# Last stage of a fused transformer layer: the router's products laid between another product's blocks, and the order of VectorE's work behind them

## What is computed

```python
x = x + ao
xf = _rms(x, n2_w).reshape(-1, C)
logits = jnp.nan_to_num(xf @ gate_w.T)
probs = jax.nn.softmax(logits, axis=-1)
topv, topi = jax.lax.top_k(probs, K)                 # K = 2 of E = 4
topv = topv / (topv.sum(-1, keepdims=True) + 1e-08)
wts = jnp.zeros((N, E), x.dtype).at[jnp.arange(N)[:, None], topi].add(topv)
o0 = _gelu(xf @ e0_up.T) @ e0_down.T
o1 = _silu(xf @ e1_w1.T) * (xf @ e1_w2.T) @ e1_down.T
o2 = _gelu(_gelu(_gelu(xf @ e2_l1.T) @ e2_l2.T) @ e2_l3.T) @ e2_l4.T
o3 = _gelu(_gelu(xf @ e3_down.T) @ e3_up.T) @ e3_out.T
moe = wts[:, 0:1] * o0 + wts[:, 1:2] * o1 + wts[:, 2:3] * o2 + wts[:, 3:4] * o3
```

## Time and profile before

| what | value |
|---|---|
| time, median of 3 runs | 5092.77 us (5092.59 to 5112.78) |
| span of the profiled execution | 5116.3 us |
| mean granted TensorE clock | 0.934 of full speed |
| busy share of the span: TensorE, VectorE, ScalarE, GpSimd | 93%, 78%, 56%, 5% |
| the last stage | about 4380 to 5116 us |

### The profile page before, as it was taken

The page is one execution under the profiler, slowest core; times in us unless marked ns, Lnnn a source line. Parts: engine busy times, 40 slices in busy tenths (PEclk is TensorE's granted clock), DMA queues, the critical chain, the costliest instruction groups (busy, mean ns, idle before and its releaser), DMA issues.

```text
span 5116.3 us, 82733 instructions
## 1 busy us (share of the span) xinstructions
PE 4781.3 (93%) x31872; PEld 2539.4 (50%) x31872; DVE 4006.1 (78%) x9075; ACT 2867.2 (56%) x3349; POOL 241.8 (5%) x259
## 2 busy tenths in 40 slices
PE   6699997868999999999999999999999999899999
PEld 5455555754434344433334433334443333688888
DVE  8677775767898988888888989988899875555555
ACT  4356554433566766666666667666567677332232
POOL 5200001110000000000000000000000000300000
PEclk9799898877899999999999999999899999899999
DMA  6622223765000201200300300300300000210010
GB/s 192 175 77 69 65 51 105 230 221 97 16 11 14 48 16 32 43 9 5 50 13 21 58 9 5 50 13 20 54 11 8 9 7 7 71 42 21 21 42 9
DMA packets 259185, 258.36 MB, mean 50 GB/s; under 512 B 78288, under 2 KB 198096, under 8 KB 257440
## 3 DMA queue, kind: packets, MB, share of 16 engines
q1 hardware_dynamic: 250784, 212.86, 14.8%
q0 software_dynamic: 6240, 38.80, 4.7%
q10 hardware_dynamic: 1768, 1.42, 0.2%
HBM read 145.44 MB, written 105.97 MB: 49 GB/s over the span
## 4 chain that ended last, share of the span: by engine, by line
PE 73%; DVE 19%; issue 5%; ACT 2%; SPq 1%; DMA 1%; DVEq 0%; ACTq 0%
PE psum L885 24%; PE psum L813 20%; PE psum L76 14%; DVE maxes_dense L951 11%; PE psum L845 4%; PE psum L777 3%; PE psum L802 2%; PE psum L823 1%; PE psum L854 1%; PE psum L1656 1%; DVE masked_scores_dense L944 1%; PE psum L809 1%; PE psum L1636 0%; PE psum L864 0%; ACT probs_dense L908 0%
## 5 line engine op out<-in xcount | busy, mean ns | idle before, releaser
L908 ACT ACTIVATE probs_dense<-psum 128x1024 f32<-128x1024 f32 (+3 forms) x2304 | 2068.1, 950 | 1042.2 <-PE psum L845 755.1
L951 DVE TENSOR_REDUCE maxes_dense<-psum 128x1 f32<-128x512 f32 x3584 | 2227.5, 684 | 232.1 <-PE psum L813 231.3
L813 PE MATMUL psum<-keys,queries_dense 48*128 48x512 f32 (+3 forms) x4608 | 1553.0, 477 | 114.6 <-DVE maxes_dense L951 22.1
L813 PEld LDWEIGHTS psum<-keys,queries_dense 48*128 48x128 f32 x4608 | 668.2, 191 | 1471.4 <-DVE maxes_dense L951 1143.6
L885 PE MATMUL psum<-probs_dense,values 128*32 128x512 f32 (+3 forms) x9216 | 1181.2, 591 | 0.0
L845 PE MATMUL psum<-queries_dense,keys 50*128 50x512 f32 (+3 forms) x4608 | 809.7, 407 | 11.5 <-ACT probs_dense L908 11.2
L944 DVE CUSTOM_DVE_ANT_0 masked_scores_dense<-psum,causal_add 128x128 f32<-128x128 f32 (+3 forms) x1024 | 452.4, 488 | 151.5 <-PE psum L813 132.2
L845 PEld LDWEIGHTS psum<-queries_dense,keys 50*128 50x128 f32 x4608 | 449.6, 193 | 106.4 <-ACT probs_dense L908 60.0
L944 DVE CUSTOM_DVE_ANT_0 masked_scores_sparse<-psum,after_add 128x512 f32<-128x512 f32 x512 | 326.2, 687 | 99.9 <-PE psum L802 99.0
L1763 ACT ACTIVATE activated<-psum 128x512 f32<-128x512 f32 x208 | 124.4, 598 | 417.5 <-PE psum L76 405.8
L885 PEld LDWEIGHTS psum<-probs_dense,values 128*32 128x32 f32 x9216 | 189.9, 109 | 273.1 <-issue 203.0
(11 more groups left out here) (296 smaller groups left out, 5252.6 us busy)
## 6 DMA issues: line engine op xcount, KB each, us to landing
v_scratch<-ve_s SPq DMA_DIRECT2D x96, 256.0 KB, 3.5
queries_dense<-parts_scratch SPq DMA_DIRECT2D x384, 64.0 KB
keys<-parts_scratch POOLq DMA_DIRECT2D x42, 512.0 KB, 18.0
parts_scratch<-part_high SPq DMA_DIRECT2D x16, 1024.0 KB, 4.3
parts_scratch<-part_low SPq DMA_DIRECT2D x16, 1024.0 KB, 7.1
values<-v_scratch POOLq DMA_DIRECT2D x8, 2048.0 KB, 35.3
queries_sparse<-parts_scratch SPq DMA_DIRECT2D x192, 64.0 KB
own_keys<-parts_scratch SPq DMA_DIRECT2D x192, 64.0 KB
```

The lines of the kernel that those rows point to most:

```text
L813: m = pe.matmul(bank[:, 0:width], q[rows(h, TROWS), h // 2, b * P:(b + 1) * P], k[rows(h, TROWS), h // 2, kc * STRIP:kc * STRIP + width], ...
L908: act.activation(probs[i % 6][:, :, first_col:STRIP], psum[:, at2:at2 + 2, first_col:STRIP], ACT.Exp, scale=SCALE, **extra).then_inc(exp_d ...
L951: m = dve.tensor_reduce(mx[:, h * BLOCKS + b, kc:kc + 1], bank, AX.X, ALU.max)
```

## The change

- TensorE: `router` becomes `router(s, b)`, one block of 6 matmuls. `expert_out(s, 2)` calls it for the next strip behind each of its four blocks. Block 0 waits for `xft_split`.
- PSUM: the router's results go to `router_bank`, which is bank 0, the first half of `turn_bank`. The router has no entry in `o_order` any more, so its wait for an output bank is gone and the experts' blocks follow one another in the two output banks.
- Semaphores: the router's last block counts `end_turned` up, which so gets 4 counts for each strip where it had 3; the waits on it are counted anew. `combine` on TensorE waits for `logit_ready` of the strip before where it waited for `xft_split`.
- VectorE: `router` is cut in two. `router_logits` (three instructions, up to `logit_ready`) stays ahead of `expert_out` 3; `router_weights` (the rest) comes behind it. The instructions are the same. For strip 0 the order is as it was.

```diff
-        turn_bank = psum[:, 0:2, :]
+        turn_bank, router_bank = psum[:, 0:2, :], psum[:, 0, :]
...
-            o_order += [(2, s, b) for b in range(BLOCKS)]
-            if s + 1 < STRIPS:
-                o_order.append(("router", s + 1, 0))
-            o_order += [(3, s, b) for b in range(BLOCKS)]
+            o_order += [(e, s, b) for e in (2, 3) for b in range(BLOCKS)]
...
                 if s >= 1:
-                    pe.wait_ge(xft_split, s)
+                    pe.wait_ge(logit_ready, s)
                 turn(ao2)
...
-            def router(s):
-                k = o_at["router", s, 0]
-                pe.wait_ge(xft_split, s + 1)
-                pe.wait_ge(o_freed, k - 1)
-                for b in range(BLOCKS):
-                    m = products(pe, o_bank(k)[:, b * EXPERTS:(b + 1) * EXPERTS], lambda l, c: xft[l][:, c, b * P:(b + 1) * P],
-                                 lambda r, c: w["gate_w"][r][:, c, :], DC)
-                m.then_inc(o_filled, 1)
+            def router(s, b):
+                if b == 0:
+                    pe.wait_ge(xft_split, s + 1)
+                m = products(pe, router_bank[:, b * EXPERTS:(b + 1) * EXPERTS], lambda l, c: xft[l][:, c, b * P:(b + 1) * P],
+                             lambda r, c: w["gate_w"][r][:, c, :], DC)
+                if b == BLOCKS - 1:
+                    m.then_inc(end_turned, 1)
...
                              lambda r, c: w[name][r][:, c, :], HC).then_inc(o_filled, 1)
+                    if e == 2 and s + 1 < STRIPS:
+                        router(s + 1, b)
...
-            router(0)
+            for b in range(BLOCKS):
+                router(0, b)
...
                 expert_out(s, 2)
-                if s + 1 < STRIPS:
-                    router(s + 1)
                 expert_out(s, 3)
...
-            def router(s):
-                k, weights = o_at["router", s, 0], wts[s % 2]
+            def router_logits(s):
                 big = 3.4028234663852886e38
+                dve.wait_ge(end_turned, 4 * s + 4)
+                chain.then(dve.tensor_scalar(logit[:].rearrange("p b e -> p (b e)"), router_bank[:, 0:BLOCKS * EXPERTS],
+                                             big, -big, ALU.min, ALU.max))
+                chain.settle()
+                chain.then(dve.tensor_reduce(red[:, :, 0], logit[:], AX.X, ALU.max))
+                chain.settle()
+                dve.tensor_tensor(logit[:], logit[:], bcast(red[:, :, 0], EXPERTS), ALU.subtract).then_inc(logit_ready, 1)
+
+            def router_weights(s):
+                weights = wts[s % 2]
                 flat = "p b e f -> p (b e f)"
-                dve.wait_ge(o_filled, k + 1)
-                dve.tensor_scalar(logit[:].rearrange("p b e -> p (b e)"), o_bank(k)[:, 0:BLOCKS * EXPERTS],
-                                  big, -big, ALU.min, ALU.max).then_inc(o_freed, 1)
-                dve.wait_ge(o_freed, k + 1)
-                chain.then(dve.tensor_reduce(red[:, :, 0], logit[:], AX.X, ALU.max))
-                chain.settle()
-                dve.tensor_tensor(logit[:], logit[:], bcast(red[:, :, 0], EXPERTS), ALU.subtract).then_inc(logit_ready, 1)
                 dve.wait_ge(prob_ready, s + 1)
...
                 expert_out(s, 2)
                 if s + 1 < STRIPS:
-                    router(s + 1)
+                    router_logits(s + 1)
                 expert_out(s, 3)
+                if s + 1 < STRIPS:
+                    router_weights(s + 1)
```

More of the change, by code:

```diff
@@ L1584, in _build @@
         hid_at = lambda s, layer: hids[(len(layers) * s + layer) % 3]
-        o_order = [("kept", 0, 0), ("kept", 0, 1), ("proj", 0, 0), ("proj", 0, 1), ("router", 0, 0)]
+        o_order = [("kept", 0, 0), ("kept", 0, 1), ("proj", 0, 0), ("proj", 0, 1)]
         for s in range(STRIPS):
@@ L1606, in load_end @@
                 if s >= 1:
-                    sp.wait_ge(end_turned, 3 * (s - 1) + 1)
+                    sp.wait_ge(end_turned, 4 * (s - 1) + 1)
                 sp.dma_start(ao2[:], rows_of(ao_d[2], s)).then_inc(ao2_in, 16)
@@ L1612, in load_end @@
                 if s >= 1:
-                    sp.wait_ge(end_turned, 3 * (s - 1) + 2)
+                    sp.wait_ge(end_turned, 4 * (s - 1) + 2)
                 sp.dma_start(ao1[:], rows_of(ao_d[1], s)).then_inc(ao1_in, 16)
@@ L1732, in combine @@
             def combine(s):
-                act.wait_ge(end_turned, 3 * s + 1)
+                act.wait_ge(end_turned, 4 * s + 1)
                 if s >= 1:
@@ L1736, in combine @@
                 act.activation(a2t[:], turn_bank, ACT.Copy).then_inc(features_set, 1)
-                act.wait_ge(end_turned, 3 * s + 2)
+                act.wait_ge(end_turned, 4 * s + 2)
                 if s >= 1:
@@ L1744, in high_norm @@
             def high_norm(s):
-                act.wait_ge(end_turned, 3 * s + 3)
+                act.wait_ge(end_turned, 4 * s + 3)
                 if s >= 1:
                     act.wait_ge(h_done, per_h * (s - 1) + first_h[5])
-                    act.wait_ge(o_filled, o_at["router", s - 1, 0] + 1)
+                    act.wait_ge(end_turned, 4 * s)
                 act.activation(xft[0][:], turn_bank, ACT.Copy).then_inc(features_set, 1)
@@ L1804, in combine @@
                 if s >= 1:
-                    dve.wait_ge(end_turned, 3 * s)
+                    dve.wait_ge(end_turned, 4 * s - 1)
                 for b in range(BLOCKS):
@@ L1825, in low_norm @@
                 dve.tensor_tensor(xft[1][:], turn_bank, xft[0][:].bitcast(F32), ALU.subtract).then_inc(xft_split, 1)
-            def router(s):
-                k, weights = o_at["router", s, 0], wts[s % 2]
+            def router_logits(s):
                 big = 3.4028234663852886e38
-                flat = "p b e f -> p (b e f)"
-                dve.wait_ge(o_filled, k + 1)
-                dve.tensor_scalar(logit[:].rearrange("p b e -> p (b e)"), o_bank(k)[:, 0:BLOCKS * EXPERTS],
-                                  big, -big, ALU.min, ALU.max).then_inc(o_freed, 1)
-                dve.wait_ge(o_freed, k + 1)
+                dve.wait_ge(end_turned, 4 * s + 4)
+                chain.then(dve.tensor_scalar(logit[:].rearrange("p b e -> p (b e)"), router_bank[:, 0:BLOCKS * EXPERTS],
+                                             big, -big, ALU.min, ALU.max))
+                chain.settle()
                 chain.then(dve.tensor_reduce(red[:, :, 0], logit[:], AX.X, ALU.max))
@@ L1837, in router @@
                 dve.tensor_tensor(logit[:], logit[:], bcast(red[:, :, 0], EXPERTS), ALU.subtract).then_inc(logit_ready, 1)
+            def router_weights(s):
+                weights = wts[s % 2]
+                flat = "p b e f -> p (b e f)"
                 dve.wait_ge(prob_ready, s + 1)
@@ L1917, in experts_dve @@
             low_norm(0)
-            router(0)
+            router_logits(0)
+            router_weights(0)
             for s in range(STRIPS):
```

## The result

The changed kernel takes 5119.43 us (median of 20 runs, 5099.65 to 5139.6) against 5095.66 us for the kernel before (20 runs, 5071.83 to 5122.38). The ratio is 1.0034, with a 95% interval of 1.0020 to 1.0048: slower by 10 to 24 us, 17 by the ratio (the medians alone lie 23.8 apart), and within the 0.5% that the prediction calls no change. 5119.43 lies in the prediction's whole range (5074 to 5121), but above the forecast's own (5090 to 5112), at the lower end of what rival B was to give (5119 to 5127).

A forecast was written before the change was run, and what follows sets the result against it. TensorE's timeline, its idle time and clock, was taken to bound the stage. Boundaries save 17.8 us with the clock up, falls add 7.4 each at 3 or 4: +8 on 5092.77 gives 5101, own range 5090 to 5112, whole 5074 to 5121.

The forecast's parts named there:

- rival B: Clock down at nearly every boundary, six or seven of seven: +26.6 to +34 us, 5119 to 5127; chance 0.16.
- Step 1: Expert 3's wait at a boundary goes with the banks read in turn: four blocks take 5.36 not 7.69, 2.33 us saved.
- Step 2: Expert 2's third block no longer waits for VectorE's reading of the first: 0.28 us saved a boundary.
- Step 3: New TensorE wait for xft_low before the first router block, behind expert 2's first block: 1.30 us lost a boundary.
- Step 4: The router's 24 instructions keep their 2.68 us on TensorE: cost 0, bounds -0.1 and +0.2 a switch.
- Step 5: VectorE's 3.47 us weights chain, now behind expert 3, delays no TensorE product: cost 0, 2.3 us of cover.
- Step 7: TensorE's clock falls behind the new wait and thinned expert 2 blocks at 3 or 4 boundaries, 7.4 us each.
- k: Number of the seven boundaries where the clock falls; taken as half, 3 or 4, giving +4.4 or +11.8 us.
- price of 0.48 for a slow microsecond: Each microsecond of slow TensorE clock lengthens a boundary by 0.48 us, from the fourth and sixth boundaries before.
- Rival A: No or one clock fall, only idle time counting: -17.8 to -10.4 us, 5075 to 5082; chance 0.22.
- C: The weights chain reaches TensorE: 7 times up to 3.47, +24 us on top of Rival A, 5099 to 5107; chance 0.07.
- D: Expert 3's wait stays because something other than the router chain held it: +7 us, 5100; chance 0.05.

The follow-up runs named there:

- e7: e3_later with VectorE's eight rank comparisons made four times over, lengthening the weights chain; 5073.89 us in a single run.
- e8: e3_later with VectorE's eight rank comparisons made seven times over, lengthening the weights chain further; 5111.95 us in a single run.
- e4_together: The changed kernel with all four router blocks together behind expert 2's last block, VectorE's new order and the other bank kept; 0.9966 of the kernel before.
- e5_pair: The changed kernel with router blocks one expert block later, the last two side by side behind expert 2's fourth block; 5109.31 us in a single run.
- e2_wide: The changed kernel with every router matmul multiplying 192 columns of expert weights in place of 4, the wait kept; 5108.80 us in a single run.
- e3_later: The changed kernel with each router block placed one expert block later, the last behind expert 3's first block; 0.9933 of the kernel before.
- e1_fill: The changed kernel with expert 2's first block computed twice at each boundary, filling the wait for xft_low; 0.9965 of the kernel before.

## Why the prediction was right, step by step

The mechanism and each wait were right. The size was low: +8, against 14.5 in the trace and 10 to 24 in the times. The median 5119.43 is 18.4 above the 5101 forecast: 2.9 because the kernel before now takes 5095.66 where its first three runs gave 5092.77, 6.5 because the boundaries lost 14.5 and not 8, and 9.0 that one profile doesn't explain.

- Step 1, expert 3's wait gone: right. From expert 3's first load to layer 0's is 4758.78 - 4753.42 = 5.36 us at a boundary with the clock up, the forecast to the digit.
- Step 2, expert 2's wait gone: right; no weight load there waits but for `xft_low`.
- Step 3, the new wait of 1.30: right (4746.72 - 4745.31 - 0.11 = 1.30).
- Step 4, the router at its old pace: right, since the pieces add up to 20.2 as forecast (20.15 to 20.21).
- Step 5, the weights chain hidden with 2.3 us of cover: right; the chain ended 4762.84 - 4743.97 - 0.11 = 18.76 us after the first block began, for 18.75 forecast, and e7 and e8 measured the cover.
- Step 7, the clock: the kind was right, and both of its terms were too small. Four of seven fell, the upper of the "3 or 4"; the falls began 3.5 to 3.7 us into the boundary, where the prediction had 3 to 6. A fall cost 28.3 - 20.2 = 8.1 us where I took 7.4: its slow stretch was 17.07 us in all four, the long end of "14 to 17". I had let the clock come back after the first 3.4 us of expert 3's dense blocks; it took 4668.49 - 4662.56 = 5.9. With the measured terms the sum is -17.8 + 4 x 8.1 = +14.6, against 14.5 measured.
- Luck had a part in k. "Half of the boundaries" was chosen between two readings of the rows, not worked out, and what it is compared with is a single execution.
- The price of 0.48 for a slow microsecond held where TensorE issues without a gap: 8.1 / 17.07 = 0.47 here, (20.76 - 19.13) / 3.41 = 0.48 in e4_together, 3.28 / 6.83 = 0.48 in e5_pair. That the clock explains the spread of the boundaries before was only half of it, as the first and the second boundary before show, with the wait for expert 3's third block in each:

```profile
4477.58:4500.68 23.10, 20.97 (x148) 19.72 (x147) 11.63 (x41) 5.74 (x8) 0.00 (x0) 0.93 0.16 48
4568.54:4590.00 21.46, 20.96 (x148) 19.72 (x147) 11.63 (x41) 5.75 (x8) 0.00 (x0) 0.92 0.18 51
...
4491.02 0.19 PEld L76 LDWEIGHTS psum<-e_out_high,hid_high 128*128 128x128 f32 x1 [2.26 <-DVE xa_s L1912]
...
4581.99 0.19 PEld L76 LDWEIGHTS psum<-e_out_high,hid_high 128*128 128x128 f32 x1 [0.63 <-DVE xa_s L1912]
```

Both have one slow stretch of 3.41 us. In the first it came behind the wait, which is there in full (2.26), and cost 23.10 - 21.46 = 1.64 us. In the second it came ahead of it: TensorE's slower work ran while VectorE was at the router chain, 0.63 us of the wait were left, and the fall cost nothing. The 21.51 that the prediction worked out "with the clock up" is of this second kind. So the wait that the change takes away was also a cover under which a fall was free.

- Rival A is out for the changed kernel, by the 17.07 us rows: four boundaries fell behind 1.3 us of idle time. The rule behind it is that of the Trainium skill, "TensorE: Matmul & The Clock Gate", section "Why this matters for your kernels", that long idle gaps between bursts of matmuls lower the throughput. It would give no fall at 1.3 us, which e2_wide bears out and the changed kernel doesn't.
- Rival B is the same mechanism with more falls, and its price covers the measured median. What speaks against it is the four falls in the one profile, and an estimate from the times: at -17.8 + 8.1 for a fall, 10 to 24 us are 3.4 to 5.2 falls on average, if the kernel before had its 159.2 us in the mean too. How many boundaries fell in the other 19 runs no trace here shows.
- C and D are out: in the seven boundaries TensorE waits for no activation behind the weights chain, and expert 3's wait did go.

What stays open: why it is every second boundary that falls in this one profile. e3_later, e1_fill and e2_wide have none in seven, e5_pair one. The two rows of e5_pair show that the instructions of a boundary alone don't decide it. Whether it is the boundary's place in time, as the prediction supposed, is not shown: no run here moved a boundary in time and nothing else.

## What to carry to other kernels

When work is put between other work to take away a wait, look at what its first piece waits for: here a router lot one block too early turned a 0.3 us wait into 1.3 us, and one block later it waits for nothing. Thin matmuls (here 4 columns at the price of 192) did best one lot at a time between dense blocks and away from any wait (e3_later). Beside a wait they did worst: the wait itself cost 1.3 us, and the clock that fell with it 8.1 in four of seven boundaries. And a wait taken away can uncover what was free beneath it. The runs of this kernel lie 50 us apart, three times what the change is worth; cut the trace at the change and compare the stretches.

## What the hardware showed that I had not expected

TensorE got faster by doing more: 12 thrown-away matmuls at a boundary (e1_fill) took the seven from 173.7 to 141.5 us, since the clock no longer fell. The fall was not graded: of the changed kernel's boundaries three lost nothing and four lost 8.1 us, with the same instructions. The slow clock held for 17.07 us while TensorE issued without a gap, through the thinned work and 5.9 us of dense blocks behind it. And the same seven boundaries of e8_long6 had 2.8 to 3.0 us of idle time each, of which four ended in a fall and three didn't.
